# A chained memset of 8 columns behind every gather on GpSimd

## What is computed

```python
# layer 0: for each node its first 25 neighbours by index, maximum over their feature rows
idx   = top_k(where(adj != 0, -arange(N), -inf), 25)
agg   = max over the 25 rows x[idx]            # 0 takes part where degree <= 25
x     = layernorm(x + relu(concat(x, agg) @ W0 + b0))
# layer 1: 4 heads of 64, h = x @ W; only type 1 occurs in adj
w     = leaky_relu(e_src[i] + e_dst[j]) where adj == 1, else -1e9
x     = layernorm(x + headnorm(relu(softmax(w) @ h + bias) + h))
```

## Time and profile before

| | |
|---|---|
| median of 2 runs | 6559.18 us (6556.46 to 6561.9) |
| profiled execution: time, span | 6569.77 us, 6568.0 us |
| mean granted TensorE clock | 0.723 |
| busy share: PE, DVE, POOL, ACT | 60%: DVE; 57%: PE; 51%: POOL; 33%: ACT |
| gathers | 3200, software queue q0, 419.64 MB |
| memory traffic | 100 GB/s over the span |

### The profile page before, as it was taken

One profiled execution on the slowest core, in us unless ns is written; L12 is line 12 of the kernel. 1 busy time (PEld: TensorE's weight loads), 2 busy tenths in 40 slices (PEclk: granted clock), 3 DMA queues, 4 the chain that ended last, 5 costly groups with the idle time before them and its releaser, 6 DMA issues.

```text
span 6568.0 us, 57561 instructions
## 1 busy us (share of the span) xinstructions
PE 3758.1 (57%) x12546; PEld 1690.9 (26%) x12546; DVE 3914.1 (60%) x12445; ACT 2183.1 (33%) x4674; POOL 3318.6 (51%) x3204
## 2 busy tenths in 40 slices
PE   1222456656556556556566556566556656555687
PEld 1111222322222222223222222222222222222232
DVE  4544565665665665666566556566556656656666
ACT  3333223333333333333333333333333333333212
POOL 4666555455455455455555545545545555554500
PEclk9555667677777777776777767777767777777888
DMA  4433333333333333333333333333333333333200
GB/s 125 122 115 115 105 100 105 103 100 109 105 99 110 99 105 106 107 96 105 100 106 109 100 102 108 100 105 104 104 98 105 103 102 107 104 102 98 78 21 26
DMA packets 264399, 658.75 MB, mean 100 GB/s; under 512 B 62161, under 2 KB 128978, under 8 KB 247762
## 3 DMA queue, kind: packets, MB, share of 16 engines
q0 software_dynamic: 153600, 419.64, 22.1%
q1 hardware_dynamic: 110546, 236.66, 10.3%
HBM read 605.73 MB, written 50.33 MB: 100 GB/s over the span
## 4 chain that ended last, share of the span: by engine, by line
another core or an unknown queue 26%; DVE 24%; PE 24%; issue 20%; ACT 5%; DVEq 1%; POOL 1%; DMA 0%; SPq 0%; ACTq 0%; POOLq 0%
PE acc L1253 11%; DVE uv L832 7%; PE pB L1221 5%; DVE rmax L851 3%; DVE top L719 3%; PE acc L1179 2%; DVE key_b L721 2%; PE pB L1222 1%; ACT raw L569 1%; PE pT L1153 1%; PE pB L1237 1%; DVE rmax L860 1%; DVE key_a L721 1%; DVE stf L953 1%
## 5 line engine op out<-in xcount | busy, mean ns | idle before, releaser
L492 POOL DMA_INDIRECT rows<-in_x_dram,idx x3200 | 3318.4, 1037 | 2891.7 <-DVE rmax L851 1693.3
L1253 PE MATMUL acc<-uv,hs 128*65 128x512 f32 x4096 | 2156.8, 683 | 172.5 <-ACT raw L569 171.5
L832 DVE SCALAR_TENSOR_TENSOR uv<-rq,qinv,maskT 128x512 f32<-128x512 f32 x2048 | 1504.4, 741 | 1175.5 <-remote 674.0
L1221 PE MATMUL pB<-w_sb,xaT 128*128 128x256 f32 x1024 | 443.9, 608 | 1305.6 <-DVE pad L734 794.6
L1253 PEld LDWEIGHTS acc<-uv,hs 128*65 128x65 f32 x4096 | 622.5, 159 | 1440.8 <-issue 1396.9
L634 ACT ACTIVATE xaT<-pA 128x512 f32<-128x512 f32 x128 | 76.4, 597 | 2071.6 <-remote 1788.3
L1221 PEld LDWEIGHTS pB<-w_sb,xaT 128*128 128x128 f32 x1024 | 300.6, 308 | 1469.0 <-issue 1012.8
L732 DVE SCALAR_TENSOR_TENSOR key_b<-pB,wordkey 128x128 f32<-128x128 f32 x128 | 36.7, 287 | 914.7 <-remote 834.0
L851 DVE TENSOR_TENSOR rmax<-rmax,rows 128x1280 f32<-128x1280 f32 x384 | 569.7, 1484 | 7.0 <-DMA rows<-in_x_dram,idx 4.4
L1231 PE MATMUL pA<-id,xh 128*128 128x128 f32 x256 | 81.6, 418 | 811.7 <-DVE xh L814 432.9
L643 ACT ACTIVATE x1T<-pA 128x256 f32<-128x256 f32 x128 | 49.2, 384 | 1089.5 <-PE pA L1231 979.2
(11 more groups left out here) (116 smaller groups left out, 4509.4 us busy)
## 6 DMA issues: line engine op xcount, KB each, us to landing
adj_sb<-in_adj_dram SPq DMA_DIRECT2D x128, 1024.0 KB
rows<-in_x_dram,idx POOLq DMA_INDIRECT x3200
xh_dram<-xh SPq DMA_DIRECT2D x128, 256.0 KB
xr<-xh_dram SPq DMA_DIRECT2D x64, 512.0 KB
xt<-in_x_dram SPq DMA_DIRECT2D x128, 128.0 KB
out_dram<-xr SPq DMA_DIRECT2D x32, 512.0 KB, 2.9
w_sb<-in_L_gnn_W_dram SPq DMA_DIRECT2D x1, 512.0 KB
wcat<-in_L_gnn_W_dram SPq DMA_DIRECT2D x2, 128.0 KB
```

The costliest lines, as they stand in the source:

```text
L492: nc.gpsimd.indirect_dma_start(rows[:, c, r * C:(r + 1) * C], None, x_rows, bass.IndirectOffsetOnAxis(ap=idx[u][:, k:k + 1], axis=0)).then ...
L832: stt = nc.vector.scalar_tensor_tensor(uv[k][:, i, :], rq[i][:], inv, m, ALU.max, ALU.mult)
L1221: nc.tensor.matmul(p_lin, xaT[:, c, :], w0_sb[:, c, :], start=(c == 0), stop=False)
L1253: last = nc.tensor.matmul(acc[i][0:HW, :], hs[:, (1 - quad.par) * JT + jt, h, :], uv[k][:, i, :], start=(jt == 0), stop=(jt == JT - 1))
```

## The change

Behind each gather GpSimd runs a memset of a new tile `idle`, 128 partitions of 8 f32 columns that nothing reads. The memset increments `s_pace`, and GpSimd waits for that count before it goes on, to the next gather or the next chunk's wait. At the end of each tile the semaphore is cleared. The gathers, their order, buffers and semaphores stay.

```diff
+        idle = sb("idle", [P, 8], F32)
...
+        s_pace = sem("s_pace")
...
                 for v in quad.reach(lambda q: QT * q + u + 1):
                     pool.wait_ge(s_idx, v)
+                pace = Chain(pool, s_pace)
                 for c in range(CH):
 
                     for v in quad.reach(lambda q: CH * (QT * q + u) + c + 1):
...
                         nc.gpsimd.indirect_dma_start(
                             rows[:, c, r * C:(r + 1) * C], None, x_rows,
                             bass.IndirectOffsetOnAxis(ap=idx[u][:, k:k + 1], axis=0)).then_inc(s_rows[c], 16)
+                        pace.then(nc.gpsimd.memset(idle[:], 0.0))
+                pace.end()
```

## The result

| | before | after |
|---|---|---|
| median | 6559.18 us | 5603.49 us (5598.51 to 5608.47, 2 runs) |
| ratio | 1 | 0.854, 95% interval 0.851 to 0.858 |
| profiled span | 6568.0 us | 5596.7 us |
| mean granted TensorE clock | 0.723 | 0.738 |

The change makes the kernel 14.6% faster; slower was forecast. On a later occasion the changed kernel took 5593.79 us against 6587.59 us, ratio 0.849 (0.847 to 0.852).

The account below looks back on a forecast made before the run. It took a chain through the gather batch to bound the kernel before, and GpSimd after the change: 45.3 + 128 x 52.5 + 357.5 = 7123 us of span, so about 7110 us, 8.4% slower; range 5600 to 7650 us.

Parts of the forecast that it names:

- What bounds the kernel before: Chain of gather batch, late release of TensorE's reports, VectorE's search and L851: 48.2 us a tile, GpSimd idle 13.2.
- The memset itself: New memset on GpSimd behind each gather: 0.11 us long, starting 0.15 us after the gather ends.
- The wait: GpSimd's wait for the memset before every next gather: 0.80 us, since nothing is prepared ahead.
- The sum for one gather: GpSimd, start to start: 1.04 + 0.15 + 0.11 + 0.80 = 2.10 us against 1.34; bounds 1.48 to 2.26.
- decision point of 1.93: 48.2 / 25 = 1.93 us between gather starts: below, GpSimd can't be the bound; above, relief of TensorE can't help.
- GpSimd as the bound: GpSimd's batch of 25 gathers grows to 52.5 us, over the tile's 48.2, and sets the time; chance 0.50.
- the rule for the run: Whole span: 45.3 us before the first gather, 128 tiles, 357.5 us after the last; 7123 us at 52.5 a tile.
- The remote waits: Waits of VectorE and ScalarE for TensorE's reports would shrink but gain nothing, lying beside GpSimd's batch.
- short waits, and the pauses free TensorE: Rival: gathers cost 1.48 to 1.63 us, pauses release TensorE's reports, 41 us a tile, 5650 us, 14% faster; chance 0.24.
- The release stays tied to the batch's end: Rival: pauses free nothing, TensorE's reports wait for the longer batch's end; 7260 us (0.10) or about 9000 (0.07); chance 0.17.
- Hidden: Rival: memsets fit in GpSimd's 13.2 us of idle time a tile, time stays at 6560 us; chance 0.09.
- What would show it: Trace signs: gather spacing 2.10 us, L851 waits from 1693 us to nearly nothing, row waits on L851, L634's lag changed.

Follow-up runs that it names:

- plain: The kernel before with nothing changed, run again for a trace on a later occasion: 5103.32 us, ratio 1.000.
- e_mid: Kernel before plus one memset and wait behind each chunk's third gather, then an unread semaphore increment so the wait stands alone: 5751.95 us, ratio 0.870.
- m_two: Kernel before plus one memset and wait behind each chunk's third gather, the wait carried by the next gather: 6464.97 us, ratio 0.977.
- m_three: Three chained memsets, each waited for, behind every gather in place of the changed kernel's one: 6488.23 us, ratio 0.996 against the kernel before.
- m_nowait: Changed kernel's memset behind every gather, but waited for only at the start of the next tile: 6676.51 us, ratio 1.008 against the kernel before.
- w_self: Kernel before, no memset; behind every gather GpSimd's queue increments a semaphore itself and waits for it: 6686.04 us, ratio 1.011.
- m_lag1: Changed kernel with each memset waited for one gather later, and all 25 at the tile's end: 6673.79 us, ratio 1.009 against the kernel before.
- m_chunk: Changed kernel with memset and wait kept only behind each chunk's fifth gather: 5639.01 us, ratio 0.866 against the kernel before.
- m_inner: Changed kernel with memset and wait only between gathers of one chunk, none at its end: 6211.0 us, ratio 0.938 against the kernel before.

## Why the prediction was wrong, point by point

- **What bounds the kernel before** was read rightly: reports of TensorE that come late while gathers follow one another, and at once when gathering pauses. It was a reading of four tiles; the records of increments confirm it (89 of 124 for xaT more than 1 us late), plain, with the same gathers and none of it, puts a number to it (1456 us), and e_mid against m_two shows that a pause cuts it. What the reading lacked is that it sets in during the batch and depends on a condition of the chip. A slip: the gather at 3166.60 under which TensorE came free is the twelfth of tile 66; it is the maximum above it that belongs to tile 65.
- **The memset itself**: 0.11 us forecast, 0.121 measured. Its start behind the gather was taken as 0.15 us and was 0.00, which is 3.8 us a tile too much, but by itself wouldn't have turned the forecast: 25 x 1.95 = 48.8 us is still over 48.2.
- **The wait: this is the step that failed.** 0.80 us was taken for every gather; measured in the median are 0.27 us on twenty of the 25, 0.88 on four and 1.06 on the last, 0.42 in the mean of all, so 25 x 0.38 = 9.5 of the 11.9 us a tile that the forecast was too long. The step was "the upper row is the nearer: same engine, same instruction, an empty queue". The row was the earlier trace rows's 0.81 us, and that gather stood behind the wait for its buffer, which is an instruction of its own. Behind a wait that the gather carries itself it starts after 0.27 us, so the price of 0.81 belonged to the kind of the wait and not to the gather. That "nothing is prepared ahead if the queue stops at the wait" was right only for the five gathers a tile at which the new wait meets the old one.
- **The sum for one gather** was 2.10 us; measured is 40.6 / 25 = 1.62 in the mean, with the gather itself at 1.08 (1.04 forecast). That is within the bounds recorded (1.48 to 2.26) and below the decision point of 1.93.
- **GpSimd as the bound, and the rule for the run** held. 45.3 + 128 x 40.6 + 357.5 = 5600 us against a measured span of 5596.7; m_three, at 1.90 us a gather, lands within 2% of the kernel before, as the decision point of 1.93 has it.
- **The remote waits** were expected to shrink and bring nothing. They vanished, and with GpSimd at 41 us a tile they brought everything: a tile was 48.2 us.
- **The rival that came true** is "short waits, and the pauses free TensorE", 5650 us forecast and 5603 measured. The argument set against it, that 0.30 us between gathers doesn't free TensorE, was true (m_nowait, w_self, m_lag1) but beside the point: the gaps that the change makes are longer than 0.30 us, and those at the chunks' ends do most of it (m_chunk). That its time meets the measured one is partly luck: it rests on at most 25 x 1.63 = 41 us, with 0.59 us behind every gather, where the trace has 0.39 us behind twenty and 1.00 and more behind five, and it put GpSimd just off the bound, where the trace has it on the bound. The rule of the Trainium skill ("Perfetto Trace Analysis", section "DMA Instruction — SWDGE (GPSIMD)") that such a DMA is decoded and put into a wait queue before its semaphore comes agrees with the 0.27 us. The 0.89 us at the chunk's end is where it doesn't help, since there the wait isn't the DMA's own.
- **The other rivals.** "The release stays tied to the batch's end" is what m_nowait, w_self and m_lag1 show (1.008 to 1.011) and isn't what the change does. Its 9000 us has a slip: it adds the 19 us to every tile and not to three of four, which would be 62.5 us a tile and some 8400 us. "Hidden" fell with the remote waits.
- **What would show it**, as recorded, did: 1.34 us inside a chunk, GpSimd's wait for L851 down from 1693 us to nearly nothing, waits for rows on L856, L639 right behind its transposes.

## What to carry to other kernels

Before a wait is priced by a row, ask whether that row's wait was carried by the instruction or stood ahead of it: here 0.27 us against 0.89 us, with the same engine and the same operation. When a wait has no releaser in the profile and ends just behind another engine's stretch of work, price its removal as a gain of its own, since it can outweigh the cost of the edit; then find the few places where a gap does it (two a tile gave 12 to 14%, against 15% for 25). The records of increments decide it where the list of waits only says "remote". And run the kernel before beside each version, on more than one occasion: here its time moved from 6559 to 5103 us with nothing changed, and an edit worth 15% on the one occasion would, by the estimate above, have cost some 10% on the other.

## What the runs showed of the hardware that I had not expected

- While GpSimd prepared gathers back to back, increments of semaphores by TensorE reached ScalarE some 14 us late (xaT "remote" 1788 us over 89 waits; by the records of increments 14.4 us in the median and at most 28.4); in plain, with the same instructions, none of those for xaT or key_b came more than 0.02 us late.
- Five gaps a tile of 0.93 us from gather to gather, with the wait ahead of the gather, cut the hold-up to 1.3 us in the median for key_b (e_mid 5752 us); gaps of 0.39 us with the wait carried by the gather do so only in part (8.0 us in m_two, 6465 us; 3.1 us in m_inner, 6211 us); gaps of 0.72 us, also carried, did in m_three (0.2 us); gaps of 0.30 us with no open wait not at all (m_nowait 6677 us).
- A memset of one or eight columns on GpSimd takes 0.12 us alone, starts at the gather's end, and is free inside the 0.30 us between gathers (m_nowait: 1.25 us from start to start). Eighteen in a row of one column took 0.61 to 0.75 us.
- An increment that nobody reads, put between a wait and a gather, costs some 0.54 us of gap (0.81 against 0.27), since it takes the wait from the gather.
